# Graph layer front: eight adjacency row tiles mirrored across the diagonal, or two opposite square blocks a step without mirrors

## The chip, the cores and the metric

The kernel runs on one core of a Trainium2 chip. The core has five engines with instruction streams of their own: TensorE (PE in the profile; its weight loads are PEld), VectorE (DVE), ScalarE (ACT), GpSimd (POOL) and SyncE (SP, which issues the DMAs here). They meet only at semaphores. SBUF is the working memory of 128 partitions, PSUM the eight banks that TensorE writes. The metric is the device time of one execution in microseconds.

## The reference, cut to what matters

```
h = relu(layernorm(x))                       # x: 8 x 2048 x 128, f32
HW = einsum('bnf,fo->bno', h, W)             # W: 128 x 128
A_norm = relu((A + A.T) * 0.5)               # A: 2048 x 2048, f32
D = sum(A_norm, axis=1)
DAD = D**-0.5 [:, None] * A_norm * D**-0.5 [None, :]
out = x + relu(einsum('nm,bmo->bno', eye - DAD, HW))
```

So the symmetric matrix S = relu(A + A.T) and all its row sums must be there before the first product with it, since each of its entries is scaled by the degrees.

## The kernel before, in words

The whole of S stays in SBUF as 16 row tiles of 128 x 2048 f32 (`S[:, n, :]`). A **unit** is one half of the batch (4 of 8) and one tile of 128 nodes, 128 x 512 elements, so there are 32 units; units 0 to 15 are the first half. The kernel has two parts.

**The front** builds S. The adjacency comes by SP as 16 whole row tiles of 1 MB (L201), each partition's piece being 8 KB long; the 256 KB units of x come as four pieces of 512 B a partition (L183), six of them ahead of the first row tile and then one behind each. A **job** is a piece of up to 4 blocks of 128 x 128 of row tile n on or below the diagonal. TensorE turns the opposite blocks of the rows that are there (`turn_adj`, L527), VectorE adds them to the piece in place (`add_transposed`, L387), ScalarE clips it and sums its rows on the way (`relu_s`, L303). The part above the diagonal is the mirror of what has been clipped: TensorE turns it again (`turn_mirror`, L539), ScalarE copies it into place (`take_mirror`), either whole (L311), in which case VectorE sums its rows (`sum_mirror`, L393), or block by block with the sums (L316). A table, `plan`, puts a job's mirror three jobs behind it, so a row tile can be worked off as soon as it lands. PSUM gives two banks to jobs and two to mirrors.

Between the jobs, VectorE makes the layer norm statistics of one unit a slot (`statistics`, L372 and L375), GpSimd turns them into a mean and a root and writes the normalised unit (`normalise`: seven small operations, of which the power at L239, and four of 128 x 128 at L253). `statistics(u)` waits until GpSimd has normalised unit u - 5 or so (`LN_SLOTS` is 6), and it stands in VectorE's row in front of the next additions. Four units are split into two f16 parts in the front (`split_h_hi` L322 on ScalarE, `split_h_lo` L380 on VectorE).

Then comes the **degree chain**: VectorE sums the partial degrees (L462), adds the diagonal to four tiles (`take_diag`, L398), takes the maximum through a turn on TensorE (L550, L473) and ends with the scales `dneg` and `dpos` (L491, L492).

**The main part** splits the pieces of S into f16 parts, in place (`split_l_hi` L331 on ScalarE, `split_l_lo` L402 on VectorE), and multiplies (L561 to L563): 8 stages of 16 row tiles, twelve matmuls of 128 x 512 a row tile, a step of the loop being called tau. In the first stage step tau also needs unit tau's split, and those splits run three steps ahead. Behind each stage come the products with W (L575 to L577), VectorE's `take_product` (L415), GpSimd's `add_x` (L271) and the store.

Of the kernel before, what the change touches and what calls it, by code (L numbers as in the profile page):

```python
# [12 lines left out]
P = 128  # L13
GRP = 4
# [5 lines left out]
X_EARLY = 6  # L20
DVE_SUMMED = (0, 1, 3)
MIRROR_LAG = 3
LN_SLOTS = 6
# [6 lines left out]
H_EARLY = 4  # L30
# [3 lines left out]
def gnn_layer(nc, x, adj, w, out):  # L34
# [12 lines left out]
    jobs = [(n, g, GRP if g < n // GRP else n % GRP + 1) for n in range(T) for g in range(n // GRP + 1)]  # L47
    mirrors = [j for j, (n, g, k) in enumerate(jobs) if n != GRP * g]
    mirror_no = {j: q for q, j in enumerate(mirrors)}
    mirror_blocks = [k - (n // GRP == g) for n, g, k in jobs]  # L50
    plan, pending = [[] for _ in range(T)], []
    for j, (n, g, _) in enumerate(jobs):
        plan[n].append(("job", j))
        if j in mirror_no:
            pending.append(j)
        if len(pending) > MIRROR_LAG:
            plan[n].append(("mirror", pending.pop(0)))
    plan[T - 1] += [("mirror", j) for j in pending]


    h_slot = [2 * u + 3 for u in range(H_EARLY)] + [T + u - H_LEAD for u in range(H_EARLY, T)]
    h_slot += [T + 12 + 3 * k for k in range(T)]
    stat_slot = [max(0, u - 3) if u < X_EARLY else u for u in range(T)]
    stat_slot += [h_slot[T + k] - 4 for k in range(T)]
# [4 lines left out]
    h_order = [u for slot in range(T + STEPS) for u in h_at.get(slot, [])]  # L69
    assert h_order == list(range(HALVES * T))  # L70
# [4 lines left out]
    adj_v = adj.rearrange("(t p) m -> t p m", p=P)  # L75

    with ExitStack() as ctx:
# [20 lines left out]
        lnt = sb("lnt", [P, 2, 4, GRP])  # L98
        mhalf = sb("mhalf", [P, GRP])
# [8 lines left out]
        deg_part = xn[:, 1, 0:T * (G + T)].rearrange("p (t c) -> p t c", t=T)  # L108
# [22 lines left out]
        adj_in = [sem(f"adj_in{n}") for n in range(T)]  # L131
# [12 lines left out]
        m_turned = sem("m_turned")  # L144
        m_taken = sem("m_taken")
        m_summed = sem("m_summed")
        zeroed = sem("zeroed")
# [32 lines left out]
        def _(sp):  # L180
# [15 lines left out]
            load_x(0)  # L196
            sp.dma_start(w_raw, w).then_inc(w_in, 16)
            for u in range(1, X_EARLY):
                load_x(u)
# [6 lines left out]
            stored = 0  # L206
# [17 lines left out]
        def _(pool):  # L224
# [6 lines left out]
            def normalise(u):  # L231
                neg_mean, v, y, t = (lnt[:, u % 2, i, :] for i in range(4))
                at = LN_OPS * u
                pool.wait_ge(stats_ready, u + 1)
                nc.gpsimd.tensor_scalar(v, mv[:, u % LN_SLOTS, :, 1], 1.0, EPS, ALU.mult, ALU.add).then_inc(ln_chain, 1)
                nc.gpsimd.tensor_scalar(neg_mean, mv[:, u % LN_SLOTS, :, 0], -1.0, 0.0, ALU.mult,
                                        ALU.add).then_inc(ln_chain, 1)
# [11 lines left out]
                if u >= T + XN:  # L249

                    pool.wait_ge(h_lo_ready, u - XN + 1)
                for b in range(GRP):
                    last = nc.gpsimd.tensor_scalar(xn_buf(u, b, b + 1), x_buf(u, b, b + 1), neg_mean[:, b:b + 1],  # L253
                                                   y[:, b:b + 1], ALU.add, ALU.mult)
                last.then_inc(xn_ready, 1)
# [18 lines left out]
            for u in range(T):  # L274
                normalise(u)
# [3 lines left out]
            for slot in range(T, T + STEPS):  # L279
                tau = slot - T  # L280
                for u in stat_at.get(slot - 1, []):
                    if u >= T:
                        normalise(u)
# [11 lines left out]
        def _(act):  # L295
# [3 lines left out]
            def relu_s(j):  # L299
                n, g, k = jobs[j]  # L300
                act.wait_ge(a_added, j + 1)
                piece = S[:, n, g * WIDE:g * WIDE + k * P]
                nc.scalar.activation(piece, piece, ACT.Relu, accum_out=deg_part[:, n, g:g + 1]).then_inc(s_ready, 1)  # L303

            def take_mirror(j):
                n, g, _ = jobs[j]
                k, q = mirror_blocks[j], mirror_no[j]
                act.wait_ge(m_turned, q + 1)
                bank = ps[:, 2 * (q % 2) + 1, :]
                if g in DVE_SUMMED:  # L310
                    nc.scalar.activation(S[:, GRP * g:GRP * g + k, n * P:(n + 1) * P],  # L311
                                         bank[:, 0:k * P].rearrange("p (k c) -> p k c", k=k),
                                         ACT.Copy).then_inc(m_taken, 1)
                else:
                    for i in range(k):
                        last = nc.scalar.activation(S[:, GRP * g + i, n * P:(n + 1) * P], bank[:, i * P:(i + 1) * P],  # L316
                                                    ACT.Copy, accum_out=deg_part[:, GRP * g + i, G + n:G + n + 1])
                    last.then_inc(m_taken, 1)
# [21 lines left out]
            act.wait_ge(zeroed, 1)  # L340
            for slot in range(T):
                for what, j in plan[slot]:
                    if what == "job":
                        relu_s(j)
                    else:
                        take_mirror(j)
                for u in h_at.get(slot, []):
                    split_h_hi(u)
# [5 lines left out]
            for tau in range(STEPS):  # L354
                s = tau // T
                if s and tau % T < GRP:
                    split_g_hi(GRP * (s - 1) + tau % T)
                if tau + LEAD < STEPS:
                    split_l_hi(tau + LEAD)
                for u in h_at.get(T + tau, []):  # L360
                    split_h_hi(u)
# [4 lines left out]
        def _(dve):  # L366
# [16 lines left out]
            def add_transposed(j):  # L383
                n, g, k = jobs[j]
                dve.wait_ge(a_turned, j + 1)
                piece = S[:, n, g * WIDE:g * WIDE + k * P]
                nc.vector.tensor_tensor(piece, ps[:, 2 * (j % 2), 0:k * P], piece, ALU.add).then_inc(a_added, 1)  # L387

            def sum_mirror(j):
                n, g, _ = jobs[j]  # L390
                k = mirror_blocks[j]
                dve.wait_ge(m_taken, mirror_no[j] + 1)
                nc.vector.reduce_sum(deg_part[:, GRP * g:GRP * g + k, G + n],  # L393
                                     S[:, GRP * g:GRP * g + k, n * P:(n + 1) * P], AX_X).then_inc(m_summed, 1)
# [241 lines left out]
```

## Time and profile before

| | us |
|---|---|
| median of 3 runs | 450.33 |
| lowest, highest | 449.49, 450.54 |
| the profiled execution | 451.35 |
| its span, first to last instruction | 449.5 |

The profiled execution is 1.02 us above the median, and 1.85 us of it lie outside the span. The page gives TensorE 89% of the span, VectorE 43%, ScalarE 27%, GpSimd 44%. These are means over two parts with different limits, so the forty slices and the stretches are to be read first, then the chain of work that ended last, and only then the groups of instructions.

### The profile page before, as it was taken

To read this page: it belongs to the slowest core of one execution; us is meant where nothing else is said; L and a number is where in the kernel's file an instruction comes from. 1 tells how busy PE (TensorE), PEld (TensorE's weight loads), DVE (VectorE), ACT (ScalarE), POOL (GpSimd) and SP (SyncE) were. 2 spreads that over 40 slices of the span, in tenths; PEclk is the share of its full clock that TensorE was granted. 3 is DMA by queue.
4 is the path that set the end of the run, shared out by engine and by line. 5 is a ranking of instruction groups with operands and counts; after the bars stand their busy time and mean duration, and the time that the engine had idled before them with its cause. 6 is when DMAs were issued, how large, how long until landed. Compare 5 with 4: busy or idle time off the path is not lost.

```text
span 449.5 us, 5973 instructions
## 1 busy us (share of the span) xinstructions
PE 399.9 (89%) x2179; PEld 207.2 (46%) x2179; DVE 194.9 (43%) x525; ACT 123.6 (27%) x284; POOL 197.4 (44%) x399
## 2 busy tenths in 40 slices
PE   0275666399999999999999999999999999999994
PEld 0164555144445444544454445554444444444442
DVE  5468897898327753866476111121111111111111
ACT  1165798484124333423343011000000000000000
POOL 5888886507708985698576001321211121111111
PEclk9998899589999999999999999999999999999999
DMA  8999970054002300320033003331111111111101
GB/s 257 422 391 389 385 195 1 1 140 142 0 2 69 111 8 1 115 76 0 1 93 95 0 1 93 95 93 48 47 48 47 48 47 48 47 49 47 48 24 47
DMA packets 53166, 42.40 MB, mean 94 GB/s; under 512 B 1808, under 2 KB 51088, under 8 KB 51088
## 3 DMA queue, kind: packets, MB, share of 16 engines
q1 hardware_dynamic: 53136, 42.02, 28.8%
q8 instruction: 17, 0.28, 0.3%
q14 instruction: 13, 0.11, 0.1%
HBM read 33.62 MB, written 8.39 MB: 93 GB/s over the span
## 4 chain that ended last, share of the span: by engine, by line
issue 40%; PE 31%; POOL 14%; DVE 5%; DMA 4%; ACT 3%; SPq 2%; POOLq 0%; DVEq 0%
PE ps L561 10%; PE ps L562 10%; PE ps L563 10%; POOL sums L271 6%; DMA S<-in_adj_dram 4%; POOL hbuf L253 2%; POOL lnt L239 2%; ACT S L303 1%; DVE S L387 1%; POOL dsv L262 1%; ACT S L311 1%; DVE stats L372 1%; SPq L183 1%; POOL xn L253 1%; DVE xn L393 1%
## 5 line engine op out<-in xcount | busy, mean ns | idle before, releaser
L562 PE MATMUL ps<-S,hbuf 128*128 128x512 f16 x512 | 195.1, 381 | 0.0
L561 PE MATMUL ps<-S,hbuf 128*128 128x512 f16 x496 | 188.0, 379 | 0.0
L563 PE MATMUL ps<-S,hbuf 128*128 128x512 f16 x496 | 188.0, 379 | 0.0
L271 POOL TENSOR_TENSOR sums<-res,sums 128x512 f32<-128x512 f32 x32 | 40.9, 1281 | 199.0 <-DVE res L415 199.0
L337 ACT ACTIVATE g<-ps 128x512 f16<-128x512 f32 x32 | 19.1, 597 | 223.9 <-PE ps L563 187.7
L562 PEld LDWEIGHTS ps<-S,hbuf 128*128 128x128 f16 x512 | 50.3, 98 | 57.1 <-issue 1.0
L563 PEld LDWEIGHTS ps<-S,hbuf 128*128 128x128 f16 x496 | 48.5, 98 | 58.5
L561 PEld LDWEIGHTS ps<-S,hbuf 128*128 128x128 f16 x496 | 48.5, 98 | 54.9
L407 DVE SCALAR_TENSOR_TENSOR g<-ps,g 128x512 f16<-128x512 f32 x32 | 22.0, 686 | 118.0 <-ACT g L337 118.0
L415 DVE SCALAR_TENSOR_TENSOR res<-ps,dsv 128x512 f32<-128x512 f32 x32 | 22.1, 692 | 88.1 <-PE ps L577 88.1
L402 DVE SCALAR_TENSOR_TENSOR S<-S,dneg 128x512 f16<-128x512 f32 x62 | 49.4, 811 | 0.3
L331 ACT ACTIVATE S<-S,dneg 128x512 f16<-128x512 f32 x62 | 43.4, 715 | 21.5 <-DVE S L402 21.5
L527 PE MATMUL ps<-ident,S 128*128 128x128 f32 x136 | 27.2, 324 | 23.2 <-DMA S<-in_adj_dram 16.8
L239 POOL TENSOR_TENSOR lnt<-lnt,mhalf 128x4 f32<-128x4 f32 x32 | 34.5, 1078 | 0.0
L253 POOL TENSOR_SCALAR xn<-hbuf,lnt 128x128 f32<-128x128 f32 x64 | 33.7, 540 | 1.7
L303 ACT ACTIVATE S<-S 128x512 f32<-128x512 f32 (+3 forms) x40 | 22.7, 567 | 33.3 <-DVE S L387 33.2
L527 PEld LDWEIGHTS ps<-ident,S 128*128 128x128 f32 x136 | 18.9, 166 | 27.3 <-DMA S<-in_adj_dram 12.4
L539 PE MATMUL ps<-ident,S 128*128 128x128 f32 x120 | 23.1, 316 | 8.9 <-ACT S L311 5.3
L253 POOL TENSOR_SCALAR hbuf<-hbuf,lnt 128x128 f32<-128x128 f32 x64 | 29.1, 469 | 1.7
L372 DVE BATCH_NORM_STATS2 stats<-hbuf 128x6 f32<-128x128 f32 x128 | 27.6, 277 | 1.0 <-DMA hbuf<-in_x_dram 1.0
L387 DVE TENSOR_TENSOR S<-ps,S 128x512 f32<-128x512 f32 (+3 forms) x40 | 23.5, 597 | 8.0 <-PE ps L527 8.0
L575 PE MATMUL ps<-w,g 128*128 128x128 f16 x128 | 23.1, 219 | 1.4 <-DVE g L407 1.4
(68 smaller groups left out, 303.9 us busy)
## 6 DMA issues: line engine op xcount, KB each, us to landing
S<-in_adj_dram SPq DMA_DIRECT2D x16, 1024.0 KB, 13.1
hbuf<-in_x_dram SPq DMA_DIRECT2D x32, 256.0 KB, 5.0
sums<-in_x_dram SPq DMA_DIRECT2D x32, 256.0 KB, 2.8
out_dram<-sums SPq DMA_DIRECT2D x32, 256.0 KB, 2.3
res<-in_L_gnn_W_dram SPq DMA_DIRECT2D x1, 64.0 KB, 2.7
```

The costliest lines, as they stand in the source:

```text
L239: nc.gpsimd.tensor_tensor(y, v, mhalf[:], ALU.pow).then_inc(ln_chain, 1)
L253: last = nc.gpsimd.tensor_scalar(xn_buf(u, b, b + 1), x_buf(u, b, b + 1), neg_mean[:, b:b + 1], y[:, b:b + 1], ALU.add, ALU.mult)
L271: nc.gpsimd.tensor_tensor(sums[:, e % SUMS, :], res[:, e % 2, :], sums[:, e % SUMS, :], ALU.add).then_inc(sum_ready, 1)
L303: nc.scalar.activation(piece, piece, ACT.Relu, accum_out=deg_part[:, n, g:g + 1]).then_inc(s_ready, 1)
L331: nc.scalar.activation(l_hi(t), s_piece(t), ACT.Copy, scale=dneg[:, mt:mt + 1]).then_inc(l_hi_ready, 1)
L372: nc.vector.bn_stats(stats[:, u % 2, b, :], x_buf(u, b, b + 1)).then_inc(stats_raw, 1)
L387: nc.vector.tensor_tensor(piece, ps[:, 2 * (j % 2), 0:k * P], piece, ALU.add).then_inc(a_added, 1)
L402: nc.vector.scalar_tensor_tensor(l_lo(t), s_piece(t), dneg[:, t % T:t % T + 1], l_hi(t), ALU.mult, ALU.subtract).then_inc(l_lo_ready, 1)
L527: last = nc.tensor.transpose(ps[:, 2 * (j % 2), i * P:(i + 1) * P], S[:, GRP * g + i, n * P:(n + 1) * P], ident[:])
L561: nc.tensor.matmul(acc, hbuf[:, u, 0, cols], l_hi(t), start=(mt == 0), stop=False)
L562: nc.tensor.matmul(acc, hbuf[:, u, 0, cols], l_lo(t), start=False, stop=False)
L563: last = nc.tensor.matmul(acc, hbuf[:, u, 1, cols], l_hi(t), start=False, stop=(mt == T - 1))
```

## The change

The adjacency is cut into a 4 x 4 grid of square blocks of 512 x 512. A **step** takes the blocks (i, j) and (j, i), or one block on the diagonal, so there are ten steps: (0,0), (0,1), (1,1), (0,2), (1,2), (2,2), (0,3), (1,3), (2,3), (3,3). A step has 4 tiles of 128 x 512 on the diagonal and 8 off it, 64 in all. Every tile is turned, added and clipped by itself; `turn_mirror`, `take_mirror`, `sum_mirror`, the table `plan` and the clearing of `deg_part` are gone. Since the two blocks overwrite each other's sources, the additions of a step wait for all its turns (`first_tile[s + 1]`), and tile k of a step uses PSUM bank k, so its turn waits for the addition that last used that bank.

SP issues W first and then step by step the one or two blocks, 1 MB each, now in pieces of 2 KB, with two units of x behind each of the first five steps and the last six behind the last block. Units 0 to 9 get their statistics in the front, two behind each of the steps 1 to 5; units 10 to 15 get them in the main part at tau 0, 2 and 4. Only unit 0 is split in the front, behind the last tile; units 1, 2 and 3 at tau 0, the others three steps ahead as before. GpSimd normalises two units at a time with small operations of 128 x 8 in place of two sets of 128 x 4 (`LN_BATCH`), in four slots. Ahead of the scales one tile gets its diagonal in place of four.

```
-    for n in range(T):
-        sp.dma_start(S[:, n, :], adj_v[n]).then_inc(adj_in[n], 16)
-        if n >= X_EARLY:
-            load_x(n)
+    for s, (i, j) in enumerate(steps):
+        load_adj(i, j)
+        if i < j:
+            load_adj(j, i)
+        for u in range(T):
+            if x_step[u] == s:
+                load_x(u)
...
+    x_step = [0, 0, 1, 1, 2, 2, 3, 3, 4, 4, 9, 9, 9, 9, 9, 9]
+    stat_slot = [s + 1 - FRONT for s in x_step[:10]] + [0, 0, 2, 2, 4, 4]
+    h_slot = [max(0, u - H_LEAD) if u >= H_EARLY else -1 for u in range(T)]
...
+            def relu_s(s, k):
+                r, j = tiles[s][k]
+                act.wait_ge(a_added, first_tile[s] + k + 1)
+                piece = S[:, r, j * WIDE:(j + 1) * WIDE]
+                nc.scalar.activation(piece, piece, ACT.Relu, accum_out=deg_part[:, r, j:j + 1]).then_inc(s_ready, 1)
...
+            def add_transposed(s, k):
+                r, j = tiles[s][k]
+                dve.wait_ge(a_turned, first_tile[s + 1])
+                piece = S[:, r, j * WIDE:(j + 1) * WIDE]
+                nc.vector.tensor_tensor(piece, ps[:, k, :], piece, ALU.add).then_inc(a_added, 1)
...
-                for what, j in plan[slot]:
-                    if what == "job":
-                        add_transposed(j)
-                    elif j in dve_sums:
-                        waiting.append(j)
-                    if len(waiting) > 1:
-                        sum_mirror(waiting.pop(0))
+            for s in range(len(steps)):
+                for k in range(len(tiles[s])):
+                    add_transposed(s, k)
+                for u in stat_at.get(s - FRONT, []):
+                    statistics(u)
+                for u in h_at.get(s - FRONT, []):
+                    split_h_lo(u)
...
-            for mt in range(GRP):
-                take_diag(mt)
+            take_diag(0)
...
+            def turn_adj(s, k):
+                r, j = tiles[s][k]
+                before = [p for p in range(s) if k < len(tiles[p])]
+                if before:
+                    pe.wait_ge(a_added, first_tile[before[-1]] + k + 1)
+                for q in range(GRP):
+                    last = nc.tensor.transpose(ps[:, k, q * P:(q + 1) * P], S[:, GRP * j + q, r * P:(r + 1) * P], ident[:])
+                last.then_inc(a_turned, 1)
```

On TensorE, at the fifth and sixth row tile of the front, stands before (L527 turns for a job, L539 for a mirror):

```order
L527 MATMUL ps<-ident,S 128x128 [waits a_added,adj_in4]
L527 MATMUL ps<-ident,S 128x128 x3
L539 MATMUL ps<-ident,S 128x128 [waits s_ready]
L527 MATMUL ps<-ident,S 128x128 [waits a_added]
L527 MATMUL ps<-ident,S 128x128 [waits a_added,adj_in5]
```

and now, on the same engine from the first step to the second (L484 is every turn, `adj_in0_1` the landing of block (0,1)):

```order
L484 MATMUL ps<-ident,S 128x128 [waits adj_in0_0,ident_ready]
L484 MATMUL ps<-ident,S 128x128 x15
L484 MATMUL ps<-ident,S 128x128 [waits a_added,adj_in1_0,adj_in0_1]
L484 MATMUL ps<-ident,S 128x128 x3
L484 MATMUL ps<-ident,S 128x128 [waits a_added]
```

The turns have gone from small sets that wait for ScalarE and VectorE in turn to runs of 16 and 32 that wait for a landing and for VectorE alone.

On VectorE, in the second half of the front, stands before (L372 and L375 are statistics, L387 additions, L393 row sums of mirrors):

```order
L387 TENSOR_TENSOR S<-ps,S 128x512 [waits a_turned]
L372 BN_STATS stats<-hbuf 128x6 [waits xn_ready,x_in11]
L372 BN_STATS stats<-hbuf 128x6 x3
L375 BN_AGGR mv<-stats 128x2 [waits stats_raw] x4
L387 TENSOR_TENSOR S<-ps,S 128x512 [waits a_turned]
L393 TENSOR_REDUCE xn<-S 128x4 [waits m_taken]
```

and now (L364 additions, L349 and L352 statistics):

```order
L364 TENSOR_TENSOR S<-ps,S 128x512 [waits a_turned] x8
L349 BN_STATS stats<-hbuf 128x6 [waits xn_ready,x_in4]
L349 BN_STATS stats<-hbuf 128x6 x3
L352 BN_AGGR mv<-stats 128x2 [waits stats_raw] x4
L349 BN_STATS stats<-hbuf 128x6 [waits xn_ready,x_in5]
```

The row sums are gone from VectorE, eight additions stand in a row, and the wait for GpSimd (`xn_ready`) comes once a step, for a unit much further back.

From the last step into the main part VectorE has now (L357 is the split of unit 0 and then of units 1 to 3, L417 the sum of the degrees, L368 `take_diag`, L372 `split_l_lo`):

```order
L364 TENSOR_TENSOR S<-ps,S 128x512 x28
L357 SCALAR_TENSOR_TENSOR hbuf<-hbuf 128x512
L417 TENSOR_REDUCE xn<-xn 128x16
...
L372 SCALAR_TENSOR_TENSOR S<-S,dneg 128x512
L357 SCALAR_TENSOR_TENSOR hbuf<-hbuf 128x512 x3
L368 SCALAR_TENSOR_TENSOR S<-ident,dminus,S 128x128
L349 BN_STATS stats<-hbuf 128x6 x4
L352 BN_AGGR mv<-stats 128x2 x4
L349 BN_STATS stats<-hbuf 128x6 x4
```

The split of unit 0 has moved between the last addition and the sum of the degrees, and splits and statistics of other units have moved into the first steps of the main part.

## Rows read from the trace of the kernel before

**Rows 1.** The page, forty slices of the span: TensorE's clock, DMA rate.
```profile
PEclk9998899589999999999999999999999999999999
GB/s 257 422 391 389 385 195 1 1 140 142 0 2 69 111 8 1 115 76 0 1 93 95 0 1 93 95 93 48 47 48 47 48 47 48 47 49 47 48 24 47
```

**Rows 2.** Stretches: length; busy PE, PEld, DVE, ACT, POOL; clock, DMA share, GB/s.
```profile
56.00:74.00 18.00, 12.89 (x100) 10.49 (x98) 16.76 (x56) 15.86 (x62) 14.67 (x42) 1.00 0.47 126
88.00:93.00 5.00, 5.00 (x14) 1.87 (x13) 5.00 (x10) 4.28 (x8) 0.45 (x1) 0.55 0.09 18
93.00:158.00 65.00, 65.00 (x338) 30.94 (x337) 41.23 (x113) 25.74 (x42) 36.82 (x68) 1.00 0.28 80
```

**Rows 3.** Waits of TensorE from 87.7 us on: us in total, times, longest.
```profile
PE ps L575 <- DVE g L407: 1.4, 1, 1.4
```

**Rows 4.** The chain of work that ended last, in the front: start, us, what.
```profile
56.45 1.75 POOL hbuf L253 x4
58.76 0.97 POOL lnt L239
60.96 1.75 POOL hbuf L253 x4
```

**Rows 5.** Timeline: four landings that TensorE waited for, and their turns.
```profile
12.33 0.45 PE L527 MATMUL ps<-ident,S 128*128 128x128 f32 x1 [7.29 <-DMA S<-in_adj_dram]
14.72 0.69 PE L527 MATMUL ps<-ident,S 128*128 128x128 f32 x2 [1.94 <-DMA S<-in_adj_dram]
28.23 1.11 PE L527 MATMUL ps<-ident,S 128*128 128x128 f32 x4
31.54 0.66 PE L527 MATMUL ps<-ident,S 128*128 128x128 f32 x4
```

**Rows 6.** Timeline: turns on TensorE in close order, at two speeds.
```profile
42.86 1.06 PE L527 MATMUL ps<-ident,S 128*128 128x128 f32 x4
43.71 1.06 PE L539 MATMUL ps<-ident,S 128*128 128x128 f32 x4
...
46.50 0.60 PE L527 MATMUL ps<-ident,S 128*128 128x128 f32 x4
46.93 0.61 PE L539 MATMUL ps<-ident,S 128*128 128x128 f32 x4
```

**Rows 7.** Groups by line and shape up to 81.6 us: count, busy us, mean ns.
```profile
L387 DVE TENSOR_TENSOR S<-ps,S 128x512 f32<-128x512 f32 x28 | 18.7, 674 | 3.5 <-PE ps L527 3.5
L393 DVE TENSOR_REDUCE xn<-S 128x4 f32<-128x512 f32 x20 | 13.5, 682 | 2.0 <-ACT S L311 1.6
L303 ACT ACTIVATE S<-S 128x512 f32<-128x512 f32 x28 | 17.7, 633 | 17.6 <-DVE S L387 17.6
L239 POOL TENSOR_TENSOR lnt<-lnt,mhalf 128x4 f32<-128x4 f32 x16 | 16.2, 1010 | 0.0
```

**Rows 8.** Timeline, VectorE: two additions in a row, and statistics of two units.
```profile
73.96 1.28 DVE L387 TENSOR_TENSOR S<-ps,S 128x512 f32<-128x512 f32 x2
...
7.32 0.84 DVE L372 BATCH_NORM_STATS2 stats<-hbuf 128x6 f32<-128x128 f32 x4
8.36 0.84 DVE L372 BATCH_NORM_STATS2 stats<-hbuf 128x6 f32<-128x128 f32 x4
```

**Rows 9.** Timeline: degree chain to the first matmul, and a split on ScalarE.
```profile
81.71 0.49 DVE L462 TENSOR_REDUCE xn<-xn 128x16 f32<-128x320 f32 x1
82.67 0.48 PE L550 MATMUL ps<-ident,gmax 128*128 128x128 f32 x1 [2.60 <-DVE gmax L467]
82.73 1.14 DVE L398 SCALAR_TENSOR_TENSOR S<-ident,dminus,S 128x128 f32<-128x128 f32 x4
86.60 2.40 DVE L402 SCALAR_TENSOR_TENSOR S<-S,dneg,spare 128x512 f16<-128x512 f32 x2 [0.72 <-ACT spare L331]
87.61 0.61 PE L561 MATMUL ps<-spare,hbuf 128*128 128x512 f16 x1 [4.46 <-DVE S L402]
...
89.66 0.61 ACT L322 ACTIVATE hbuf<-hbuf 128x512 f16<-128x512 f32 x1
```

More of the change, by code:

```diff
@@ L44, in gnn_layer @@
     assert (HALVES, F, w.shape[1]) == (2, P, P)
[L47 to L64, printed above, removed]
+    steps = [(i, j) for j in range(G) for i in range(j + 1)]
+    tiles = [[(GRP * j + k, i) for k in range(GRP)] + [(GRP * i + k, j) for k in range(GRP if i < j else 0)]
+             for i, j in steps]
+    first_tile = [sum(len(t) for t in tiles[:s]) for s in range(len(steps) + 1)]
+    FRONT = len(steps)
+    x_step = [0, 0, 1, 1, 2, 2, 3, 3, 4, 4, 9, 9, 9, 9, 9, 9]
+    stat_slot = [s + 1 - FRONT for s in x_step[:10]] + [0, 0, 2, 2, 4, 4]
+    h_slot = [max(0, u - H_LEAD) if u >= H_EARLY else -1 for u in range(T)]
+    h_slot += [12 + 3 * k for k in range(T)]
+    stat_slot += [h_slot[T + k - k % LN_BATCH] - 5 + k % LN_BATCH for k in range(T)]
     h_at, stat_at = {}, {}
@@ L129, in s_piece @@
             return S[:, t % T, (t // T) * WIDE:(t // T + 1) * WIDE]
-        adj_in = [sem(f"adj_in{n}") for n in range(T)]
+        adj_in = [[sem(f"adj_in{i}_{j}") for j in range(G)] for i in range(G)]
         w_in = sem("w_in")
@@ L229, in _, with normalise @@
                                     pattern=[[-1, P]], channel_multiplier=1).then_inc(ident_ready, 1)
[L231 to L237, printed above, removed]
+            def normalise(first):
+                k = first // LN_BATCH
+                slot = first % LN_SLOTS
+                neg_mean, v, y, t = (lnt[:, k % 2, i, :] for i in range(4))
+                mean, var = (mv[:, slot:slot + LN_BATCH, :, i].rearrange("p u b -> p (u b)") for i in range(2))
+                at = LN_OPS * k
+                pool.wait_ge(stats_ready, first + LN_BATCH)
+                nc.gpsimd.tensor_scalar(v, var, 1.0, EPS, ALU.mult, ALU.add).then_inc(ln_chain, 1)
+                nc.gpsimd.tensor_scalar(neg_mean, mean, -1.0, 0.0, ALU.mult, ALU.add).then_inc(ln_chain, 1)
                 pool.wait_ge(ln_chain, at + 1)
@@ L248, in normalise @@
                 pool.wait_ge(ln_chain, at + 7)
[L249 to L255, printed above, removed]
+                for u in range(first, first + LN_BATCH):
+                    if u >= T + XN:
+                        pool.wait_ge(h_lo_ready, u - XN + 1)
+                    for b in range(GRP):
+                        c = (u - first) * GRP + b
+                        last = nc.gpsimd.tensor_scalar(xn_buf(u, b, b + 1), x_buf(u, b, b + 1), neg_mean[:, c:c + 1],
+                                                       y[:, c:c + 1], ALU.add, ALU.mult)
+                    last.then_inc(xn_ready, 1)
             def scale_rows(s):
@@ L272, in add_x @@
                                         ALU.add).then_inc(sum_ready, 1)
-            for u in range(T):
+            for u in range(0, T, LN_BATCH):
                 normalise(u)
@@ L278, in _ @@
                 scale_rows(s)
[L279 to L283, printed above, removed]
+            for tau in range(STEPS):
+                for u in stat_at.get(tau - 1, []):
+                    if u > T and u % LN_BATCH == LN_BATCH - 1:
+                        normalise(u - LN_BATCH + 1)
                 s = tau // T
@@ L359, in _ @@
                     split_l_hi(tau + LEAD)
-                for u in h_at.get(T + tau, []):
+                for u in h_at.get(tau, []):
                     split_h_hi(u)
@@ L437, in _ @@
             nc.vector.tensor_tensor(w16[:, 1, :], w_sb, w16[:, 0, :], ALU.subtract).then_inc(w_chain, 1)
[L439 to L455 removed]
+            for s in range(len(steps)):
+                for k in range(len(tiles[s])):
+                    add_transposed(s, k)
+                for u in stat_at.get(s - FRONT, []):
+                    statistics(u)
+                for u in h_at.get(s - FRONT, []):
+                    split_h_lo(u)
             D, root, y, t = (deg[:, i, :] for i in range(4))
             top, scale, unscale = (gmax[:, i:i + 1] for i in range(3))
[L459 to L461 removed]
+            dve.wait_ge(s_ready, first_tile[-1])
             nc.vector.reduce_sum(D, deg_part, AX_X).then_inc(deg_chain, 1)
```

124 lines of the change are left out of this document (24 added, 100 removed).

## The prediction

> **What bounds the kernel now.** I read the slices first, then stretches, then the chain of waits, and only then single instructions. The main part is TensorE's own time. From 93 to 158 us it is busy for 65.00 of 65 us at full clock [rows 2], and from the first matmul at 87.61 us [rows 9] to the end it waits only once, for 1.4 us [rows 3]. None of these matmuls is changed. So what the change is worth is how far it moves the point 87.61 us, less what the main part then loses.
>
> The front has no single limit. The loads ran at 385 to 422 GB/s in the second to fifth slice and had fallen to 195 in the sixth, which ends at 67 us [rows 1], so the bytes are in well before the front ends. From 56 to 74 us VectorE is busy for 16.76 of 18 us, ScalarE for 15.86 and GpSimd for 14.67 [rows 2], and the chain runs in that stretch through GpSimd's normalising, with a period of 4.5 us a unit: its write of one unit starts at 56.45 us and that of the next at 60.96 [rows 4]. VectorE's statistics wait for it, and additions and mirrors stand behind them. ScalarE's copies of mirrors are nearly as full. The reader is to see that after the load the old front is a balance of three engines, so taking work from one alone would give little; this change takes it from all three.
>
> **The loads.** Row tiles without x between them land 2.39 us apart (14.72 less 12.33), with one unit of x between them 3.31 (31.54 less 28.23), so a unit costs 0.92; the six tiles from 12.33 to 28.23 took 2.65 each [rows 5]. Six units and one tile had landed at 12.33, which puts the start of the stream at 12.33 - 2.39 - 5.52 = 4.4 us. The change sends 512 pieces of 2 KB a block in place of 128 pieces of 8 KB. No row shows this piece. The bounds are a tile's 2.39 and four units of x, which are 1 MB in 512 B pieces, 3.68. I take 2.65: the time for a piece goes as its bytes plus something fixed, and between the two ends 2 KB lies near the large one (one quarter of the tile's piece, four times x's; worked out linearly, 2.6). Then blocks land at 7.1 (step 0), 14.2 (step 1), 18.7, 25.8, 33.0, 37.5, 42.8, 48.1, 53.4 and 56.0 us, with the ten units of x of steps 0 to 4 between.
>
> The DMA page of the Trainium skill ("DMA: Bandwidth & Descriptors", Specifications) gives 512 B as enough for the full rate. Rows 5 disagree for x, whose 512 B pieces cost 3.68 us a MB against 2.39. By the rule a block would cost 2.39 and the sum below come out 0.7 us less.
>
> **VectorE's row.** This becomes the limit. An addition of 128x512 lasts 674 ns [rows 7], but two in a row take 1.28 us together [rows 8], so they follow each other every 0.61. Two units of statistics take 2.1 us (7.32 to 8.36 for one) [rows 8]. Removed are the row sums, 13.5 us for the 20 large ones alone [rows 7]; added are 24 additions net (64 in place of 40, of which 28 are full size). The six units' statistics that leave the front, 6.2 us, come back in the main part.
>
> The new thing is that an addition waits for all turns of its step. Four turns in close order take 0.43 us at full clock (46.50 to 46.93) and 0.85 at half (42.86 to 43.71) [rows 6]. Step 1 starts from a landing at 14.2 us with 32 turns: 3.6 us at full clock, 6.8 at half. TensorE has been mostly idle by then and starts at the lower level, as the main part does, where the clock is 0.55 for the first 5 us and 1.00 after [rows 2]; so I take 6.0, and VectorE starts step 1 at 20.2 us. From there it never waits for a load again: step 2's block is there at 18.7, and every later one lands before the additions ahead of it are over. The sum is
>
> - 60 additions of steps 1 to 9 x 0.61 = 36.6 us
> - statistics behind steps 1 to 5, 5 x 2.1 = 10.5 us
> - gaps in which the last tiles are turned. Behind an off-diagonal step with the same banks only tile 7 is left when its bank comes free: 0.46 + 0.2 = 0.7 us, for steps 7 and 8. Behind a diagonal step (3 and 6) TensorE has tiles 3 to 7 left; at half clock 4 us, less the statistics where they cover it (steps 3 and 6 both follow statistics), 2.1 us each. In all 5.6 us. At steps 2, 4, 5 and 9 statistics or free banks cover the turns.
>
> 20.2 + 52.7 = 73 us for the last addition (rounded). ScalarE's clip runs every 0.63 us (633 ns [rows 7]) beside it and ends 0.9 later, 73.9. Then comes what the change puts on the path: the split of unit 0, 0.61 on ScalarE [rows 9] and one VectorE pass of the same size, 0.7; 75.3 us. Before, the sum of degrees started at 81.71 and the first matmul at 87.61, 5.9 us [rows 9]. The sum over 64 columns in place of 320 saves 0.3, and three of the four diagonals, 1.14 us together, leave; since the maximum also waits for the turn that ends at 82.67 + 0.48 = 83.15 [rows 9], only 0.6 of that is gained. The diagonals that have moved stand where VectorE waits for ScalarE's first split. So 5.0 us, and the first matmul at **80.4 us**, 7.2 earlier.
>
> **GpSimd.** A pair has seven small operations in place of fourteen. The power (1010 ns at four columns [rows 7]) may stay or double; a pair then takes 6.3 to 7.3 us against 9.0 for two units. The statistics of unit 8, behind step 5 at 50.3 us, need unit 4 normalised; pairs done from 27 us on put that at 47. It is covered by 3 us; if a pair took 9 us, VectorE would wait 2 to 3 us there.
>
> **The main part.** VectorE now has 6.2 us of statistics and three more splits in the first steps. Working off its row from the first matmul P: the split pieces that steps 3, 5 and 7 need are done at P + 8, + 13.4 and + 19. TensorE, at 2.6 us a step at full clock and 5.1 for the first, reaches them at P + 10.3, + 15.5 and + 20.7. So nothing is lost, but the cover is 2 us. The clock starts low again here as it did before, since TensorE still idles some 7 us ahead of it. GpSimd's pairs stand ahead of `add_x` for longer; one result buffer is spare, and I cost it at nothing.
>
> **Sum.** 451.35 - 7.2 = 444.1 us against the profiled execution, whose span is 449.5. That execution is 1.0 above the median, so 443.1 against the median.
>
> **The rivals.**
>
> *Full clock in the front.* If TensorE's turns run at the higher level from step 1 on, step 1 saves 2.3 us and steps 3 and 6 save 3.3: the last addition at 67.4 and a time of 437.5. For it: runs of 32 turns are denser than anything in the old front. Against it: the old front, in its dense middle, was at the lower level at 42.86 us and at the higher one only at 46.50 [rows 6], and the new one leaves TensorE idle for some 2 us at each pair of statistics.
>
> *Half clock throughout the front.* Turns of an off-diagonal step then take 6.8 us against 4.9 for eight additions, every step waits for them, the last addition is at 81.3 and the time 451.5, no gain. Rows 6 show 4 turns in 0.85 us in the middle of the old front. The page on TensorE ("TensorE: Matmul & The Clock Gate", Part 1) says idle time brings the lower level and sustained activity releases it; waits for landings are the case it warns of. But rows 2 show release within the first 5 us of dense work, and a TensorE that is late in this front is a dense one, so the lower level ends itself. I give it little.
>
> *The slower side: blocks load slowly.* A block is 512 rows, each read at 2 KB with 6 KB skipped; nothing in the trace reads in such strides. If a block costs what 1 MB of x costs, 3.68 us, the last block lands at 4.4 + 16 x 3.68 + 9.2 = 72.5 us, and 17 us of turns, additions, clip, split and chain stand behind it: first matmul at 89.6, 452.3 us. The point from which it decides is about 3.5 us a block. [...]
>
> *VectorE or GpSimd a little slower.* Additions every 0.67 (their full length) give 446.5; a stall for GpSimd adds 2 to 3 us; a lost cover in the main part 2. Each still ends below 449.
>
> **How the numbers follow.** Forecast as summed, with blocks at 2.39 to 3.0 us and a mixed clock: 442 to 445, chance 0.55. Full clock: 0.15. A slower engine, 445 to 449: 0.13. Half clock throughout: 0.06, about no change. Slow blocks: 0.11, of which most is above 451.7. A change under 0.3%, 1.35 us, can't be told from none. So faster 0.83, same 0.06, slower 0.11. The range from 437 to 450 takes in the first three cases and leaves the last two.
>
> **What would show it.** Right: no L539-like mirrors; additions in runs 0.61 us apart; the last block landed near 56 us; the sum of degrees near 75.3 us and the first matmul near 80.4; the main part 357 us long as before, with TensorE waiting under 3 us in it. TensorE waiting for VectorE in the front is right, TensorE waiting for a landing behind step 3 is wrong and means slow blocks. Turns 0.85 us per four behind step 6 mean the half clock rival. Statistics of unit 8 waiting for GpSimd mean pairs are dear. Waits of L561's successors for splits in the first ten steps mean that the moved statistics cost what they saved.

## The result, and the profile after

The changed kernel takes 452.34 us (median of 7 runs, 451.44 to 453.76) against 449.94 for the kernel before (7 runs, 449.36 to 450.54). The ratio is 1.0045, with a 95% interval of 1.0033 to 1.0058: it is slower by 2.4 us where 7 us less was forecast. Nine microseconds lie between forecast and result, and the profile says where.

The front first, on VectorE (start, length, line, operation, count, idle time before it and what ended it). L364 is the addition.

```profile
10.17 2.48 DVE L364 TENSOR_TENSOR S<-ps,S 128x512 f32<-128x512 f32 x4 [3.97 <-PE ps L484]
20.59 4.88 DVE L364 TENSOR_TENSOR S<-ps,S 128x512 f32<-128x512 f32 x8 [7.94 <-PE ps L484]
...
34.55 4.88 DVE L364 TENSOR_TENSOR S<-ps,S 128x512 f32<-128x512 f32 x8 [2.54 <-PE ps L484]
...
55.20 4.88 DVE L364 TENSOR_TENSOR S<-ps,S 128x512 f32<-128x512 f32 x8 [2.38 <-PE ps L484]
60.83 4.88 DVE L364 TENSOR_TENSOR S<-ps,S 128x512 f32<-128x512 f32 x8 [0.75 <-PE ps L484]
66.45 7.27 DVE L364 TENSOR_TENSOR S<-ps,S 128x512 f32<-128x512 f32 x12 [0.75 <-PE ps L484]
75.19 0.69 DVE L357 SCALAR_TENSOR_TENSOR hbuf<-hbuf 128x512 f16<-128x512 f32 x1 [1.47 <-ACT hbuf L303]
75.80 0.21 DVE L417 TENSOR_REDUCE xn<-xn 128x16 f32<-128x64 f32 x1
```

This is the front as it was summed: step 1's additions start at 20.59 us (forecast 20.2), the gaps of steps 3, 6, 7 and 8 are 2.54, 2.38, 0.75 and 0.75 (2.1, 2.1, 0.7, 0.7), the sum of degrees starts at 75.80 (75.3). Then TensorE: its first matmul of the main part, and the only long wait behind it:

```profile
80.14 0.61 PE L505 MATMUL ps<-spare,hbuf 128*128 128x512 f16 x1 [3.19 <-DVE S L372]
...
125.50 0.61 PE L505 MATMUL ps<-S,hbuf 128*128 128x512 f16 x1 [6.68 <-DVE S L372]
```

The first matmul comes at 80.14 us (forecast 80.4), 7.5 earlier than the 87.61 of [rows 9]. But from there to the end of the span the kernel before needed 449.5 - 87.61 = 361.9 us, and this one needs 450.6 - 80.14 = 370.5. Of these 8.6 us, 6.68 are the wait that ends at 125.50. Most of the rest is the clock (stretch: length; busy PE, PEld, DVE, ACT, POOL; granted clock, DMA share, GB/s):

```profile
118.80:125.50 6.70, 0.02 (x2) 0.01 (x1) 1.92 (x4) 1.88 (x4) 6.26 (x13) 0.76 0.05 15
125.50:130.00 4.50, 4.50 (x13) 1.72 (x14) 4.50 (x21) 2.42 (x4) 1.72 (x4) 0.60 0.01 2
130.00:135.00 5.00, 5.00 (x25) 2.23 (x23) 2.05 (x4) 1.21 (x2) 4.56 (x11) 1.00 0.01 3
```

While TensorE waits, GpSimd is busy for 6.26 of 6.70 us, VectorE and ScalarE for 1.9 each. Behind the wait the granted clock is 0.60 for 4.5 us, mostly at the lower of its two levels, which costs 4.5 x 0.40 = 1.8 us more. Where [rows 3] had one wait of 1.4 us, there are now 6.7 and 1.4.

The chain of work that ended last tells what the wait is for (start, us, what; from the first step of the main part on, the longer pieces):

```profile
85.08 0.76 DVE stats L349 x4
85.84 0.29 DVE mv L352 x4
...
90.36 5.99 POOL hbuf L250 x8
...
100.54 5.57 POOL hbuf L250 x8
...
110.29 4.98 POOL hbuf L250 x8
115.27 2.45 POOL dsv L259 x2
...
121.14 1.76 POOL xn L250 x4
122.92 0.64 ACT hbuf L303
123.58 0.65 DVE hbuf L357
124.23 0.54 DVE S L368
124.77 0.68 DVE S L372
125.50 0.61 PE ps L505
```

For 37 us the chain runs through GpSimd: the pairs (10, 11), (12, 13) and (14, 15), whose statistics were deferred into the main part, then the two scale rows, then the first unit of the pair (16, 17). ScalarE's split of unit 16 stands at tau 12, **ahead of split piece 15 of S**, and so it does on VectorE. TensorE, which takes the first stage's last two row tiles together, does not need unit 16 before stage 4; it needs piece 15, at 118.8 us. The chain reads straight down the last five lines. The rows of ScalarE and VectorE show what each of them waited for meanwhile:

```profile
122.92 0.63 ACT L303 ACTIVATE hbuf<-xn 128x512 f16<-128x512 f32 x1 [6.98 <-POOL xn L250]
123.58 0.73 DVE L357 SCALAR_TENSOR_TENSOR hbuf<-xn,hbuf 128x512 f16<-128x512 f32 x1 [6.75 <-ACT hbuf L303]
```

### The profile page after: what moved, and what is told of

It reads as the page before. It is cut to its first block, busy times and chain, and to the rows that moved or that the text cites. A ratio compares the mean times of both kernels' runs of the same rounds, so it can differ in the third digit from the quotient of the medians.

```text
span 450.6 us, 5783 instructions
## 1 busy us (share of the span) xinstructions
PE 402.7 (89%) x2179; PEld 210.0 (47%) x2179; DVE 195.9 (43%) x519; ACT 121.6 (27%) x259; POOL 177.6 (39%) x287
## 4 chain that ended last, share of the span: by engine, by line
issue 40%; PE 29%; POOL 17%; DVE 8%; ACT 2%; DMA 2%; SPq 1%; POOLq 0%; ACTq 0%
PE ps L505 7%; PE ps L506 7%; PE ps L507 7%; POOL sums L268 6%; PE ps L484 6%; DVE S L364 4%; POOL hbuf L250 4%; DMA S<-in_adj_dram 2%; POOL lnt L234 2%; ACT S L299 2%; POOL dsv L259 2%; POOL xn L250 1%; DVE stats L349 1%; DVE hbuf L357 1%; DVE mv L352 0%
## 5 line engine op out<-in xcount | busy, mean ns | idle before, releaser
L268 POOL TENSOR_TENSOR sums<-res,sums 128x512 f32<-128x512 f32 x32 | 42.6, 1335 | 194.5 <-DVE res L385 192.5
L484 PE MATMUL ps<-ident,S 128*128 128x128 f32 x256 | 43.9, 333 | 22.0 <-DVE S L364 15.0
L372 DVE SCALAR_TENSOR_TENSOR S<-S,dneg 128x512 f16<-128x512 f32 x62 | 50.8, 830 | 0.8 <-ACT S L312 0.2
L484 PEld LDWEIGHTS ps<-ident,S 128*128 128x128 f32 x256 | 36.7, 173 | 29.3 <-issue 24.3
L299 ACT ACTIVATE S<-S 128x512 f32<-128x512 f32 x64 | 39.4, 617 | 32.2 <-DVE S L364 32.2
L364 DVE TENSOR_TENSOR S<-ps,S 128x512 f32<-128x512 f32 x64 | 39.0, 680 | 18.3 <-PE ps L484 18.3
L250 POOL TENSOR_SCALAR hbuf<-hbuf,lnt 128x128 f32<-128x128 f32 x64 | 33.9, 548 | 0.9
L231 POOL TENSOR_SCALAR lnt<-mv 128x8 f32<-128x8 f32 x16 | 6.7, 420 | 66.6 <-DVE mv L352 65.9
L234 POOL TENSOR_TENSOR lnt<-lnt,mhalf 128x8 f32<-128x8 f32 x16 | 28.9, 1807 | 0.0
L349 DVE BATCH_NORM_STATS2 stats<-hbuf 128x6 f32<-128x128 f32 x128 | 27.4, 275 | 2.3 <-POOL hbuf L250 2.3
```

What stands on the lines that cost most here:

```text
L234: nc.gpsimd.tensor_tensor(y, v, mhalf[:], ALU.pow).then_inc(ln_chain, 1)
L268: nc.gpsimd.tensor_tensor(sums[:, e % SUMS, :], res[:, e % 2, :], sums[:, e % SUMS, :], ALU.add).then_inc(sum_ready, 1)
L349: nc.vector.bn_stats(stats[:, u % 2, b, :], x_buf(u, b, b + 1)).then_inc(stats_raw, 1)
L364: nc.vector.tensor_tensor(piece, ps[:, k, :], piece, ALU.add).then_inc(a_added, 1)
L372: nc.vector.scalar_tensor_tensor(l_lo(t), s_piece(t), dneg[:, t % T:t % T + 1], l_hi(t), ALU.mult, ALU.subtract).then_inc(l_lo_ready, 1)
L484: last = nc.tensor.transpose(ps[:, k, q * P:(q + 1) * P], S[:, GRP * j + q, r * P:(r + 1) * P], ident[:])
```

## The experiments

On the wait in the main part there are two theories. **A, row order:** the late unit 16 holds up ScalarE's and VectorE's rows, and with them piece 15. **B, VectorE's load:** six statistics and three splits more in the main part make VectorE itself late. (C, in the first expectation, is a loss spread over both parts.) Two more questions follow: whether the **clock** makes the gaps of the front, and what makes GpSimd's pairs dear in the main part, VectorE's operations with two SBUF operands (**D**) or something else there (**E**). The kernel before ran beside each experiment (450.3 us in every set).

One caution for all traces below. In three kernels that change nothing in TensorE's and VectorE's front (e1_split16_later, e2_scales_behind, e8_single_units) the first matmul stands at 78.78, 77.44 and 78.07 us, against 80.14 in the changed kernel's trace: step 1's 32 turns took 5.92, 5.11 and 5.36 us there and 6.54 here. So up to 2.7 us of a difference in the first matmul can be the execution's and not the edit's.

**The splits of the second half four steps later.**

```
-    h_slot += [12 + 3 * k for k in range(T)]
-    stat_slot += [h_slot[T + k - k % LN_BATCH] - 5 + k % LN_BATCH for k in range(T)]
+    h_slot += [16 + 3 * k for k in range(T)]
+    stat_slot += [h_slot[T + k - k % LN_BATCH] - 5 + k % LN_BATCH - (4 if k < 2 else 0) for k in range(T)]
```

Units 16 and 17 keep the slots of their statistics; the later units' statistics move with their splits.

> Edit: the splits of the second half's units move four steps later (unit 16 at tau 16 in place of 12, then every three steps); statistics of units 16 and 17 stay where they are, no work is added or taken. Theory A (row order): TensorE's wait of 6.68 us in the main part ends late only because the split of unit 16, which needs GpSimd's pair (16, 17), stands ahead of split piece 15 on ScalarE and VectorE. Then the wait goes, and with it the cold matmuls behind it: 452.3 - 6.7 - 1.9 = about 444 us. Theory B (VectorE's load): the six statistics and three splits that moved into the main part make VectorE itself late; its load is unchanged here, so the wait stays near 6 us and the time near 452. Theory C (front): the loss is spread over both parts; some 448.

442.3 us (5 runs, 441.54 to 444.41), ratio to the kernel before 0.983 (0.9807 to 0.9853). In its trace the wait has shrunk to this (TensorE, the same place):

```profile
118.29 0.39 PE L505 MATMUL ps<-S,hbuf 128*128 128x512 f16 x1 [0.91 <-DVE S L372]
```

The same work in another order gives back 10 us of median and 9.0 of the profiled execution (443.38 against 452.34), 1.4 of which is an earlier first matmul (78.78). A holds. B falls as the cause: VectorE still has every operation, and although those of the later units have moved too, the changed kernel's VectorE had nothing to do for the 6.75 us up to 123.58 but to wait for ScalarE's split of unit 16, as its row above shows. The 0.91 us that are left come from the same chain: they hang on the pair (14, 15), whose unit 15 TensorE does need at this point (its split starts at 114.99 us, piece 15 is split at 118.24). So the order is mended and GpSimd is still just late.

**The scale rows behind the pair.** `scale_rows(0)` and `scale_rows(1)`, 2.48 us of GpSimd's chain, behind the pair (16, 17) in place of ahead of it.

```
-            for s in range(2):
-                scale_rows(s)
             for tau in range(STEPS):
...
                         normalise(u - LN_BATCH + 1)
+                        if u == T + 1:
+                            pool.wait_ge(d_ready, 2)
+                            for s in range(2):
+                                scale_rows(s)
```

> Edit: on GpSimd, the two scale rows (2.48 us together) move from ahead of the pair (16, 17) to behind it; nothing else. Theory A: the chain through GpSimd is shorter by just these 2.5 us, so TensorE's wait falls from 6.7 to 4.2 us and the time by 2.5, to about 449.8. Theory B: no change, 452.3.

449.5 us (447.21 to 451.14, 12 runs), 2.8 below the changed kernel where A had 2.5. From the first matmul to ScalarE's split of unit 16 there are now 118.79 - 77.44 = 41.35 us, in the changed kernel 122.92 - 80.14 = 42.78. The wait is 5.2, not 4.2: smaller, but less than dose for dose, since the first pair's seven small operations took 6.4 us in this execution and 4.1 in the other. Of the 3.7 us that the profiled executions lie apart, 2.7 are an earlier first matmul, which this edit can't have made, so the median's 2.8 is no clean measure of it either. The direction is A's, the size is not shown.

**The deferred statistics back in the front,** with the loads of their units, two a step.

```
-    x_step = [0, 0, 1, 1, 2, 2, 3, 3, 4, 4, 9, 9, 9, 9, 9, 9]
-    stat_slot = [s + 1 - FRONT for s in x_step[:10]] + [0, 0, 2, 2, 4, 4]
+    x_step = [u // 2 for u in range(T)]
+    stat_slot = [s + 1 - FRONT for s in x_step]
```

> Edit: units 10 to 15 of x are loaded two a step behind steps 5 to 7 and get their statistics in the front behind steps 6 to 8, so nothing of the front's layer norm is left for the main part. VectorE's row of the front grows by 6 x 1.04 = 6.2 us, less what fits into its gaps of 0.75 us at steps 7 and 8. Theory A: the first matmul comes 5 to 6 us later, near 85.5, and the wait in the main part goes, since GpSimd starts its pairs earlier: 452.3 + 5.3 - 8.6 = about 449, a little under the kernel before. Theory B: the same sign, since VectorE's load in the main part falls too. So it prices the deferral rather than telling A from B: if it is under 452, deferring those statistics lost more than it gained.

447.36 us (445.83 to 448.05), ratio 0.993 (0.9911 to 0.9949); first matmul at 83.98, and in the main part no wait but the one of 1.4 us that the kernel before has too. From the first matmul to the end of the span it needs 360.8 us, where the changed kernel needs 370.5. By these two traces, deferring the six statistics had bought 3.8 us in the front and lost 9.7 in the main part. B has the same sign here.

**One unit at a time.** `LN_BATCH = 1` (and the bound of the loop that calls it).

> Edit: the changed kernel with GpSimd normalising one unit at a time (seven small operations of 128x4 a unit, LN_BATCH 1) in place of two. A pair took 6.9 us in the front and 9.8 beside VectorE's splits in the main part; two single units take 2 x 4.5 = 9.0 without disturbance. Theory A: the chain through GpSimd to unit 16 has six units and then only unit 16 itself; it grows by 3 x 2.1 = 6.3 us and shrinks by nothing else, so TensorE's wait grows from 6.7 to about 12 and the time to 457 or 458: batching the pairs helped. If pairs hurt, because unit 16 has to wait for unit 17's share of the work, the time falls below 452.

456.4 us (456.06 to 458.13), and a wait of 11.98 us in the place of 6.68:

```profile
128.58 0.61 PE L505 MATMUL ps<-S,hbuf 128*128 128x512 f16 x1 [11.98 <-DVE S L372]
```

So the pairs were a good part of the change: without them GpSimd's chain is longer and the wait grows by 5.3 us. The median grows by 4.1; in the trace the first matmul came 2.1 us earlier. That is A once more, with the dose in the other direction.

**Only the early splits.** Units 0, 1 and 2 are split behind step 5, where VectorE waits for turns; the second half stays as in the change.

```
-    h_slot = [max(0, u - H_LEAD) if u >= H_EARLY else -1 for u in range(T)]
+    h_slot = [-5, -5, -5] + [max(0, u - H_LEAD) for u in range(3, T)]
```

> Edit: the changed kernel with only the splits of units 0, 1 and 2 moved behind step 5. Theory A (row order): the first matmul comes about 1.4 us earlier and VectorE has two splits less ahead of its statistics at tau 0, so GpSimd's chain starts 1.3 us sooner after it; the wait in the main part shrinks from 6.7 to about 5.4: some 449.5. Theory B (VectorE's load is what makes the main part late): three splits of nine moved operations are gone, a third of its 8.3 us, so the wait falls by 2 to 3 and the time to 448 or less.

449.91 us (446.57 to 451.21, 10 runs), with a wait of 5.66 us; A had said 449.5 and a wait of 5.4, B 448 or less and a wait of 3.7 to 4.7.

**Early and late splits together.**

> Edit: the second half's splits four steps later, as in e1_split16_later (442.3), and the splits of units 0, 1 and 2 moved behind the statistics of step 5, where VectorE waits 2.2 us for the turns of step 6. Row order theory: unit 0's split leaves the path between the last addition and the sum of the degrees (1.47 us of waiting and 0.69 of work, less the clip's end that must still be waited for, 0.7), and two splits leave the first step of the main part: 442.3 - 1.4 = about 441. If the gap at step 6 is needed for something else, the additions of step 6 start later and nothing is gained: 442.3.

440.87 us (440.35 to 442.45), ratio 0.9793 (0.9756 to 0.983). The wait of 0.91 us is gone too: the first matmul is at 76.39, and from 93 to 158 us TensorE is busy for 65.00 of 65 again, as in [rows 2].

**Extra turns in the front.** Turns of the identity, which nothing reads, in TensorE's idle time ahead of steps 1, 3 and 6.

```
+            keep = {1: (24, 0), 3: (12, first_tile[2]), 6: (12, first_tile[5])}
             for s, (i, j) in enumerate(steps):
+                if s in keep:
+                    count, added = keep[s]
+                    if added:
+                        pe.wait_ge(a_added, added)
+                    for _ in range(count):
+                        nc.tensor.transpose(ps[:, 7, 0:P], ident[:], ident[:])
```

> Edit: 24, 12 and 12 extra turns of the identity into PSUM bank 7, whose result nothing reads, in TensorE's idle time ahead of the turns of steps 1, 3 and 6; the main part is as in the changed kernel. If the clock is what makes the gaps of the front (7.94, 2.54 and 2.38 us of VectorE's waiting), the turns behind them take 3.9 us or follow the additions, the gaps fall by about 2.5, 2 and 1.8 us, and the first matmul comes about 6 us earlier, near 74; the wait in the main part stays, since its chain starts with the statistics at tau 0 and moves along: about 446. If the turns are slow for another reason (bank waits, semaphores), the first matmul stays at 80 and the time at 452.3.

The gaps fell as expected, from 7.94, 2.54 and 2.38 us to these (VectorE):

```profile
17.57 4.88 DVE L364 TENSOR_TENSOR S<-ps,S 128x512 f32<-128x512 f32 x8 [4.71 <-PE ps L484]
...
30.48 4.87 DVE L364 TENSOR_TENSOR S<-ps,S 128x512 f32<-128x512 f32 x8 [1.48 <-PE ps L484]
...
49.48 4.88 DVE L364 TENSOR_TENSOR S<-ps,S 128x512 f32<-128x512 f32 x8 [0.40 <-PE ps L484]
```

Step 1's 32 turns took 3.69 us in place of 6.54 (5.11 to 6.54 in the traces without extra turns), and the first matmul came at 74.42, 5.7 us earlier than the changed kernel's and 3.0 to 4.4 earlier than in the three traces with the same front. The wait in the main part moved along and was 7.0. So it is the clock that made most of these gaps; of step 3's, what is left has become a wait for its block, which lands at 26.75. The median is 449.14 us (447.5 to 451.18, 12 runs), 3.2 below the change; the profiled execution, 447.5, was the fastest of the twelve.

**All three edits, and then two of them.**

> Edit: e5_early_and_late with the 24, 12 and 12 extra turns of e4_warm_turns. Clock theory: the first matmul comes 5 to 6 us before e5's; if the main part has no wait that hangs on GpSimd any more, all of it shows: about 435.5. With the splits of units 0 to 2 VectorE's gap at step 6 is filled, so the turns' gain there (1.8 us) is lost in part: 436 to 437. If GpSimd's pairs are still near the path (they start with the statistics at tau 0, so they move along), the gain is as large; if the loads become the limit (step 4's blocks land at 33 to 35 us), it is 2 us smaller, 438.

440.49 us (439.07 to 440.55), where 436 to 437 was expected; the gain of the extra turns had vanished beside the early splits. I read from its trace that the three splits filled a gap which the turns had closed already, and that step 7 then began cold, and tried one split in place of three:

> Edit: e6_all_three with only unit 0 split behind step 5 (units 1 and 2 stay at tau 0). e6 gave 440.49 where 436 to 437 was expected, and its trace shows why: three splits take 1.94 us of a gap that the extra turns had closed to 0.4, and step 7's turns then start cold and leave a gap of 1.46. If that reading is right, one split costs 0.3 us there and takes 1.4 off the path behind the last addition: first matmul at 74.42 (e4) - 1.1 = 73.3 us and, with the 364.0 us that e5 needs from there to the end, 437.3 in the profiled run, some 438 as median. If the edits collide for another reason it stays at 440.5.

439.82 us (439.49 to 440.84), ratio 0.9757 (0.9722 to 0.9791). It is the lowest median of all, but not told apart from e6 and hardly from e5, and 1.8 us above what was expected. Step 7's gap is back at 0.75 us (1.46 in e6_all_three), so the reading was right about that gap and it was only a part. The first matmul stands at 75.42, not 73.3. As in the other kernels with extra turns, TensorE now waits for loads that the changed kernel never waited for (TensorE, steps 3 and 4):

```profile
27.10 3.68 PE L484 MATMUL ps<-ident,S 128*128 128x128 f32 x32 [3.03 <-DMA S<-in_adj_dram]
34.29 5.35 PE L484 MATMUL ps<-ident,S 128*128 128x128 f32 x32 [3.51 <-DMA S<-in_adj_dram]
```

Steps 3 and 4 begin at the landing of their blocks. With the gaps closed the loads are the limit up to 34 us, and what is saved ahead of them is given back. Step 4's turns were slow again behind that wait in this execution, 5.35 us, where behind the same wait they took 3.69 in e4_warm_turns and e6_all_three; these 1.7 us are most of what the first matmul missed. Why the extra turns gave 3.2 us of median alone and only 0.4 (e6 against e5) beside the early splits stays open in part; step 1's turns took 5.23 us in e5's trace, so there was less to gain than from 6.54.

> Edit: only the later splits of the second half and the extra turns, no early splits. If the gains of e1 (8.0 to 8.6) and e4 (3.2 as median, 5.7 in its profiled run) add up, the first matmul stands at 74.4 and the time is 438.5 to 439. If GpSimd's pairs come back onto the path once the front is shorter, a wait of 1 us or more shows in the main part and the time is 440 or more.

Later splits and extra turns without early splits: three runs gave 438.34, 440.55 and 442.78 us, ratio 0.9769 (0.9715 to 0.9823), too wide to say whether the two gains add up. The execution that was profiled took 1494 us, with TensorE's 128x512 matmuls at 1.10 us each in place of 0.38; why is not known, and its trace says nothing of the others. Whether GpSimd's pairs come back onto the path is answered next door: in e9_unit0_early_warm, with the first matmul at 75.42, TensorE waits 0.95 us at the place where e1_split16_later waited 0.91, so the chain moves along and is just on the path.

**What makes a pair dear.** In the front GpSimd's eight writes of a pair take 3.48 us, in the first four pairs of the main part 4.5 to 6.0. Here the additions leave out the turned block, so that both operands lie in SBUF; the output is not the reference's.

```
-                nc.vector.tensor_tensor(piece, ps[:, k, :], piece, ALU.add).then_inc(a_added, 1)
+                nc.vector.tensor_tensor(piece, piece, piece, ALU.add).then_inc(a_added, 1)
```

> The additions of the front leave out the turned block: each adds the piece of S to itself, both operands from SBUF, in place of one from PSUM and one from SBUF; the output is not the reference's. Everything else is the changed kernel. It measures why GpSimd's eight writes of a pair take 3.48 us in the front and 4.5 to 6.0 in the main part. Theory D (two SBUF operands on VectorE hold GpSimd off): the pairs' writes that run beside additions take 4.5 us or more in the front too, while those beside statistics alone stay at 3.5. Theory E (GpSimd is slowed by something else in the main part: TensorE's reads, the loads, ScalarE): they stay at 3.48. The time itself is of no use here.

GpSimd's writes of three pairs in this front, and VectorE beside two of them:

```profile
31.34 6.39 POOL L250 TENSOR_SCALAR hbuf<-hbuf,lnt 128x128 f32<-128x128 f32 x8
...
53.31 3.45 POOL L250 TENSOR_SCALAR hbuf<-hbuf,lnt 128x128 f32<-128x128 f32 x8
...
63.83 12.13 POOL L250 TENSOR_SCALAR hbuf<-hbuf,lnt 128x128 f32<-128x128 f32 x8
...
33.55 5.31 DVE L364 TENSOR_TENSOR S<-S 128x512 f32<-128x512 f32 x8 [2.27 <-PE ps L484]
...
63.55 5.11 DVE L364 TENSOR_TENSOR S<-S 128x512 f32<-128x512 f32 x8 [0.75 <-PE ps L484]
```

With VectorE idle or at statistics (from 52.3 to 57.9 us) the writes take 3.45; beside a run of additions with both operands in SBUF 6.39, and 12.13 where the runs follow each other. The one operand is all that was changed. Four stretches that hold the writes of one pair each show what does not matter (the columns are those of [rows 2]; three of the changed kernel, the last of e11_sbuf_additions):

```profile
58.70:62.20 3.50, 2.62 (x20) 1.76 (x18) 2.75 (x6) 2.90 (x11) 3.46 (x8) 1.00 1.01 273
90.40:96.30 5.90, 5.90 (x29) 2.72 (x28) 5.05 (x21) 2.48 (x4) 5.90 (x8) 1.00 0.43 126
132.80:136.30 3.50, 3.50 (x27) 1.93 (x25) 0.39 (x1) 0.33 (x1) 3.47 (x8) 1.00 0.00 0
63.80:76.00 12.20, 7.35 (x48) 5.03 (x48) 11.45 (x19) 11.00 (x35) 12.13 (x8) 1.00 0.01 3
```

The first is in the front, beside additions with one operand in PSUM, ScalarE's clips and full loads: 3.48 us. The third is in the main part, with TensorE busy throughout and VectorE nearly idle: 3.47. So neither the loads nor ScalarE nor TensorE's matmuls hold GpSimd off. D holds, E falls. The splits of S, those of the units and the diagonals (L372, L357, L368) have two SBUF operands each, and up to 129 us they are all that VectorE does in the main part beside the statistics. The Trainium skill says this too ("SBUF — State Buffer", Who interferes with whom): a VectorE instruction with two SBUF inputs contends with a GpSimd instruction that reads SBUF, and one with at most one SBUF input doesn't, outside VectorE's two-port modes. The trace agrees on both halves, 12.13 against 3.48.

## Why the prediction was wrong

**What held.** The start of the loads (7.1 and 14.2 us forecast for the first two steps, 6.83 and 14.02 in the rows of TensorE's first turns); additions 0.61 us apart; the wait for all turns of a step and its gaps; the mixed clock in the front, which the extra turns show to be the cause; the split of unit 0 on the path. The first matmul was forecast at 80.4 and came at 80.14. That it came so close is in part luck: from the sum of degrees to the first matmul it took 4.34 us where 5.0 was summed, which hid 0.5 us of lateness ahead of it, and the traces with the same front have 77.44 to 78.78. That the old front was a balance of three engines was not tested. As a sign of being right the prediction gave a main part 357 us long as before; by [rows 9] and the span it was 361.9.

**The step that failed** is the paragraph on the main part: "So nothing is lost, but the cover is 2 us." The runs showed a loss of 8.6 us in its place. The paragraph has three faults.

The first is where it stopped. VectorE's row was worked off up to step 7, as if its own load were the question (theory B), and there the sum was right: no wait of TensorE stands in those steps. The wait came at steps 14 and 15. The moved statistics were followed to VectorE's row only, although GpSimd has a pair to do behind each two of them.

The second is GpSimd's price. The forecast's "a pair then takes 6.3 to 7.3 us" was worked out from rows of the front, and in the front it is right: pairs start 6.9 us apart. In the main part the three pairs took from 86.2 to 115.3 us, 9.7 each. With 6.9 in their place, by an estimate from these rows, the chain would have reached unit 16's split at 114.6 and piece 15 some 2.5 us later, ahead of the 118.8 at which TensorE needed it, and nothing would have been lost. The trace of the kernel before had the row that warns of it, its first unit in the main part, beside VectorE's splits (start, us; GpSimd):

```profile
103.29 1.20 POOL L235 TENSOR_SCALAR lnt<-mv 128x4 f32<-128x4 f32 x1 [14.84 <-DVE mv L375]
104.73 2.10 POOL L239 TENSOR_TENSOR lnt<-lnt,mhalf 128x4 f32<-128x4 f32 x1
108.51 2.69 POOL L253 TENSOR_SCALAR xn<-hbuf,lnt 128x128 f32<-128x128 f32 x4
```

It took 103.29 to 111.20, 7.9 us, against the 4.5 of [rows 4], and it shows GpSimd idle for 14.84 us ahead of it: this idle time was the cover that the change spent. Unit 16's split stood at tau 12 in the kernel before as well, so the order did no harm as long as GpSimd was early.

The third is the order of the rows. The paragraph's "one result buffer is spare, and I cost it at nothing" looked at what GpSimd does behind its pairs; nobody was asked what stands behind the *consumer* of unit 16. A split that TensorE needs 50 steps later blocks one that it needs at once, because both are on ScalarE's row in this order. e1_split16_later shows that this order turned GpSimd's lateness into the loss: without it 0.91 us of wait are left of 6.68.

**The rivals.** Full clock in the front fell (step 1's turns took 6.54 us, at the full clock some 3.6), and so did half clock throughout (steps 7 and 8 waited 0.75 us for turns, where 6.8 us of turns against 4.9 of additions would make it 1.9 or more) and slow blocks ((14.02 - 6.83 - 2 x 0.92) / 2 = 2.7 us a block). The one in which "a lost cover in the main part" costs 2 us was the right place with a size of 8.6. No rival had the other sign there: the slower case was put on the loads, where the trace showed no sign of trouble, and not on the engine to which work had been moved.

## What to carry to other kernels

When a change moves work across a boundary between stages, write out each engine's row up to the point where the moved work is consumed, GpSimd's above all, and then ask what stands behind the consumer in its own row: in-order rows turn a result that nobody needs yet into a stall of one that is needed. A duration holds for the neighbours that it was measured beside; for an operation that moves, take the row from the stage into which it moves. Here the change was worth 2.4 us of loss as written and 8 us of gain with the second half's splits four steps later.

## What was not expected of the hardware

The same eight GpSimd writes of 128x128 took 3.45 us beside VectorE's statistics, 3.48 beside additions with one operand in PSUM and 12.13 beside additions with both in SBUF. GpSimd's power over 128x8 took 1.64 us where one over 128x4 had taken 1.01, neither constant nor double. And 24 turns that nothing reads, in 3.6 us of idle time, brought the next 32 to 3.69 us from 5.11 to 6.54. The same front, run again, varied by those 1.4 us in step 1 alone.
